# Where the next tile's query and key/value products stand in the first attention of a decoder layer

## The chip, the cores and the metric

The kernel runs on one core of a Trainium2 chip. What is measured is the device time of one execution in microseconds (us); lower is better. The core has five engines that run side by side, each through its own list of instructions in order: TensorE (PE in the profile; PEld is its weight load), VectorE (DVE), ScalarE (ACT), GpSimd (POOL) and SyncE (SP), which here issues most of the DMAs. They meet only at semaphores: an instruction can wait until a counter that other instructions raise has reached a value.

## The reference

One decoder layer on x of 16 x 64 rows of 512 numbers, in fp32: a self-attention, a cross-attention to a context, and a gated product, each followed by `layernorm(x + ...)`. The change touches the first of them only:

```
xq = rope((x @ Wq).reshape(b, 64, 32, 16))          # 32 heads of 16
xk = rope((x @ Wk).reshape(b, 64, 8, 16))           # 8 key heads, each used by 4 query heads
xv = (x @ Wv).reshape(b, 64, 8, 16)
scores = einsum('bqhd,bkhd->bhqk', xq, repeat(xk, 4)) / 4
probs  = softmax(where(causal, scores, -inf))
out    = einsum('bhqk,bkhd->bqhd', probs, repeat(xv, 4)).reshape(b, 64, 512) @ Wo
x      = layernorm(x + out)
```

`rope` turns each pair of numbers of a head by an angle that depends on the row's place.

## The kernel before

**Tiles.** The 1024 rows are cut into 8 tiles of 128 rows, two sequences of 64 each. The first attention runs one step per tile, `tile_steps(i)` for i = 0 to 7; steps 2 to 6 are a loop, the others are written out. Each of the five engines has its own `tile_steps`, and the order of calls in it is the order on that engine; nothing else orders the work. After step 7 comes a passage into the cross-attention, which the change doesn't touch.

**Precision.** Products are made in three passes: every operand is split into a high part (rounded by a ScalarE copy) and a low part (the rest, by a subtraction on VectorE or GpSimd), and high x high, high x low and low x high are summed. So each product of four 128-row chunks has 12 matmuls, and most tiles of data pass a pair of instructions, a copy named `..._high` or `copy` and a subtraction named `low`.

**Three tiles are in work at once.** Step i handles tile i up to its scores and softmax, tile v = i - 1 from its last probabilities to its output product, and tile w = i - 2 in its residual sum and layernorm. The calls that matter, by engine:

- TensorE: `b_stage` is the query product (12 matmuls of 512 columns, line 432) into bank 1, `kv_stage` the key/value product (12 of 256 columns, L413) into bank 2. `pt_stage(v, u)` turns the probabilities of unit u (0 to 3; a unit is a quarter of a tile's scores) in banks 3 and 4 (L451). `a_stage(i + 1)` turns the next x tile in bank 1 (L423). `qk_stage` turns queries and keys in six groups of four transposes (L487) that take banks 0, 3 and 4 in turn. `s_stage` makes scores, units 0 and 1 first, 2 and 3 later (L511). `pv_stage` is probabilities times values (L463), `x1_stage` turns the normed tile w (L523), `wo_stage` is the output product of tile v into bank 0 (L413, 12 matmuls of 512 columns).
- VectorE: `rope_q` (three instructions, L1317 to L1320) and `rope_k` (L1328 to L1331) read the products from banks 1 and 2. `q_low`, `p_low`, `x_low`, `at_low`, `x1_low` are subtractions that share L1300. `masked_max` is a masked copy of scores (L1382) and a maximum (L1384); `total` is a sum of exponentials (L1388) and a reciprocal. `add1(w)` (L1353) adds the output product in bank 0 to x; `stats1`, `moments1` and `norm1` are the layernorm.
- ScalarE: `p_high`, `x_high`, `at_high`, `x1_high`, the two copies that spread queries and keys over `stack_q` and `stack_k`, the copy `v_raw`, the six evictions of the turned queries and keys (semaphore `s_qke`), and `expo`, the exponentials (L876).
- GpSimd: `sub` subtracts the maximum (L1136), `norm` multiplies by the reciprocal (L1141), and two sums finish rope (L1154 for queries, semaphore `s_qs`; L1158 for keys, `s_ks`).

**Waits around the change.** `qk_stage` begins with two waits on TensorE, which hold all its six groups:

```
pe.wait_ge(s_ql, t + 1)          # q_low of this tile
if tile_stages(t)[2]:
    pe.wait_ge(s_res, t - 1)     # add1 of tile t - 2
```

The second is there because the first group of transposes writes bank 0, in which the output product of tile t - 2 lies until `add1` has read it. The second and third group wait for `p_low` of units 2 and 3, whose transposes lie in banks 3 and 4. `pt_stage` of units 2 and 3 waits for `p_low` of units 0 and 1, for the same banks. The fourth group waits for the first eviction, the fifth for the second, the sixth for the third, and the first scores for the third.

## Time and profile before

| | us |
|---|---|
| three runs | 827.94, 832.75, 835.98 |
| their median | 832.75 |
| the profiled execution | 829.94 |
| its span, first to last instruction | 828.1 |

The profiled execution is 1.8 us longer than its span. The first attention takes the first 22% of the span: its loop steps follow each other every 20.3 us, from about 57 to 159 us, and the passage into the cross-attention begins at about 180 us. The rows below are from the page of this execution and from views of its trace. A timeline row gives the start in us from the span's start, the length in us, the engine, the line, the operation, what it writes and reads, and, in brackets, how long the engine had been idle before it and what released it. Starts of instructions that follow each other on an engine are a little closer than their lengths, since one's end overlaps the next one's start.

### The profile page before, as it was taken

How to read it: one execution, taken by the hardware profiler on the slowest of the kernel's cores; microseconds unless marked ns; L12 is line 12 of the kernel's file. 1: busy time of each engine (PE TensorE's matmuls, PEld its weight loads, DVE VectorE, ACT ScalarE, POOL GpSimd, SP SyncE). 2: the span in 40 equal slices, each digit the busy share in tenths (PEclk: the TensorE clock that was granted, in tenths of full speed). 3: DMA queues.
4: the chain of work that ended last, by engine and by line, in shares of the span. 5: the costliest groups of instructions: out<-in, count | busy, mean ns of one | idle time of the engine just before them, and what ended most of it. 6: DMA issues, size and time to landing. Idle time of an engine off the chain costs nothing.

```text
span 828.1 us, 15482 instructions
## 1 busy us (share of the span) xinstructions
PE 763.8 (92%) x5504; PEld 688.7 (83%) x5504; DVE 626.5 (76%) x1172; ACT 317.2 (38%) x652; POOL 402.1 (49%) x422
## 2 busy tenths in 40 slices
PE   4689998899899999999999999999999999998792
PEld 3577777789799998999999899999989999996662
DVE  4778888877887777687777668768767876876967
ACT  4455555553443324233243324334333333322403
POOL 7566666664454445444543535454453554532124
PEclk9899999999999999999999999999999999999997
DMA  9600004012432222133122223212232221112002
GB/s 237 140 17 17 16 16 117 3 55 52 103 105 75 51 78 78 39 73 88 55 51 76 77 50 91 85 25 51 76 94 58 76 76 25 26 42 86 1 1 102
DMA packets 104047, 53.49 MB, mean 65 GB/s; under 512 B 80208, under 2 KB 89552, under 8 KB 104016
## 3 DMA queue, kind: packets, MB, share of 16 engines
q1 hardware_dynamic: 103184, 51.51, 24.1%
q10 hardware_dynamic: 576, 1.05, 0.4%
q0 software_dynamic: 256, 0.52, 0.2%
q8 instruction: 19, 0.31, 0.2%
q14 instruction: 12, 0.10, 0.0%
HBM read 32.62 MB, written 2.10 MB: 42 GB/s over the span
## 4 chain that ended last, share of the span: by engine, by line
PE 69%; DVE 16%; issue 7%; POOL 3%; ACT 2%; DMA 1%; SPq 1%; DVEq 0%; POOLq 0%
PE bank L413 30%; PE bank L640 18%; DVE arena_r L1300 4%; PE s_bank L654 4%; PE s_bank L656 2%; PE bank L463 2%; PE bank L624 2%; PE bank L487 2%; DVE small L1388 2%; DVE arena_f L1382 1%; PE s_bank L624 1%; DMA arena_f<-in_L_attn_Wo 1%; POOL arena_f L1215 1%; PE s_bank L487 1%; PE bank L633 1%
## 5 line engine op out<-in xcount | busy, mean ns | idle before, releaser
L413 PE MATMUL bank<-arena_r 128*128 128x256 f32 (+1 forms) x2580 | 354.6, 294 | 2.6 <-DVE arena_r L1300 1.8
L413 PEld LDWEIGHTS bank<-arena_r 128*128 128x128 f32 x2580 | 328.3, 191 | 18.4 <-issue 2.9
L838 ACT ACTIVATE arena_r<-bank 128x256 fp32r<-128x256 f32 (+2 forms) x251 | 105.7, 458 | 234.4 <-PE bank L607 99.1
L640 PE MATMUL bank<-arena_r 128*128 128x512 f32 x768 | 192.2, 399 | 1.1 <-DVE arena_r L1300 1.0
L640 PEld LDWEIGHTS bank<-arena_r 128*128 128x128 f32 x768 | 140.1, 189 | 28.3 <-issue 1.7
L1300 DVE TENSOR_TENSOR arena_r<-bank,arena_r 128x256 fp32r<-128x256 f32 (+2 forms) x219 | 100.8, 487 | 57.2 <-ACT arena_r L838 57.0
L838 ACT ACTIVATE arena_r<-arena_f 128x512 fp32r<-128x512 f32 (+2 forms) x177 | 103.1, 637 | 89.0 <-DMA arena_f<-arena_f 73.7
L1300 DVE TENSOR_TENSOR arena_r<-arena_f,arena_r 128x512 fp32r<-128x512 f32 (+1 forms) x113 | 114.1, 1023 | 20.7 <-ACT arena_r L838 20.7
L1182 POOL TENSOR_TENSOR arena_f<-arena_f 128x256 f32<-128x256 f32 x64 | 54.2, 847 | 91.6 <-DVE arena_f L1460 91.5
L1210 POOL TENSOR_TENSOR arena_f<-arena_f,small 128x512 f32<-128x512 f32 x32 | 33.4, 1045 | 117.2 <-DVE small L1523 117.2
L1215 POOL TENSOR_TENSOR arena_f<-arena_f,small 128x512 f32<-128x512 f32 x32 | 44.2, 1380 | 68.1 <-DVE small L1529 68.1
L1486 DVE TENSOR_TENSOR arena_f<-bank,arena_f 128x512 f32<-128x512 f32 x64 | 43.9, 685 | 25.6 <-PE bank L640 25.6
L838 ACT ACTIVATE arena_f<-s_bank 128x512 f32<-128x512 f32 (+1 forms) x34 | 20.3, 598 | 98.9 <-PE s_bank L656 96.8
L656 PE MATMUL s_bank<-arena_r 128*128 128x64 f32 x256 | 57.9, 245 | 0.0
L654 PE MATMUL s_bank<-arena_r 128*128 128x128 f32 x256 | 57.2, 295 | 0.0
L838 ACT ACTIVATE arena_r<-s_bank 128x512 fp32r<-128x512 f32 (+1 forms) x98 | 51.8, 529 | 1.0 <-PE s_bank L487 0.7
L1183 POOL TENSOR_TENSOR arena_f<-arena_f 128x256 f32<-128x256 f32 x64 | 50.1, 783 | 0.0
L656 PEld LDWEIGHTS s_bank<-arena_r 128*128 128x128 f32 x256 | 49.1, 192 | 1.2
L654 PEld LDWEIGHTS s_bank<-arena_r 128*128 128x128 f32 x256 | 49.1, 192 | 1.2
L1517 DVE TENSOR_TENSOR arena_f<-s_bank,arena_f 128x512 f32<-128x512 f32 x32 | 22.1, 692 | 36.7 <-ACT arena_f L838 36.7
L1136 POOL TENSOR_TENSOR arena_f<-arena_f,small 128x512 f32<-128x512 f32 x32 | 34.8, 1087 | 30.7 <-DVE small L1384 30.7
L1300 DVE TENSOR_TENSOR arena_r<-s_bank,arena_r 128x512 fp32r<-128x512 f32 x82 | 47.4, 580 | 1.2 <-ACT arena_r L838 0.9
(134 smaller groups left out, 1029.8 us busy)
## 6 DMA issues: line engine op xcount, KB each, us to landing
arena_f<-arena_f SPq DMA_DIRECT2D x128, 128.0 KB, 2.5
arena_f<-in_L_xattn_Wq SPq DMA_DIRECT2D x8, 1024.0 KB, 5.5
arena_f<-in_L_xattn_Wo SPq DMA_DIRECT2D x8, 1024.0 KB, 5.5
arena_f<-in_x SPq DMA_DIRECT2D x8, 256.0 KB, 2.8
arena_f<-in_x SPq DMA_DIRECT2D x1, 2048.0 KB, 16.9
arena_f<-in_L_xattn_Wk SPq DMA_DIRECT2D x8, 256.0 KB, 2.9
arena_f<-in_L_xattn_Wv SPq DMA_DIRECT2D x8, 256.0 KB, 3.2
arena_f<-in_ctx SPq DMA_DIRECT2D x8, 256.0 KB, 3.1
```

The lines of the kernel that those rows point to most:

```text
L413: mm = pe.matmul(bank, lhs(a, c), rhs(b, c), start=(c == 0 and n == 0), stop=(c == chunks - 1 and n == 2))
L640: mm = pe.matmul(BO2[i][:], at2[a][:, h, i * P:(i + 1) * P], w2o_s[b][:, h, :], start=(h == 0 and n == 0), stop=(h == HG - 1 and n == 2))
L654: pe.matmul(BS2[h][:, at:at + 2 * S], high, kT2[:, :, b * S:(b + 1) * S], start=True, stop=False, skip_group_check=True)
L656: mm = pe.matmul(BS2[h][:, at + S:at + 2 * S], low_, kT2[:, 0, b * S:(b + 1) * S], start=False, stop=True, skip_group_check=True)
L838: act.activation(dst, src, ACT.Copy).then_inc(done, 1)
L1136: pool.tensor_tensor(cut(p1[u], b=8, k=S), cut(sc1[u % 2], b=8, k=S), bcast(mx1[u], 2, S), ALU.subtract).then_inc(s_sub, 1)
L1182: pool.tensor_tensor(u1q[:, 0, j, :], u1q[:, 0, j, :], u2q[:, 1, j, :], ALU.subtract).then_inc(c_qs, 1)
L1183: pool.tensor_tensor(u1q[:, 1, j, :], u1q[:, 1, j, :], u2q[:, 0, j, :], ALU.add).then_inc(c_qs, 1)
L1210: pool.tensor_tensor(cut(p2, b=8, k=S), cut(sc2, b=8, k=S), bcast(mx2, 2, S), ALU.subtract).then_inc(c_sub, 1)
L1215: pool.tensor_tensor(cut(p2, b=8, k=S), cut(p2, b=8, k=S), bcast(sm2, 2, S), ALU.mult).then_inc(c_pn, 1)
L1300: dve.tensor_tensor(dst, src, f32(high), ALU.subtract).then_inc(done, 1)
L1486: dve.tensor_tensor(y, banks[6 + i][:], y, ALU.add).then_inc(c_acc, 1)
```

## The change

The query product of tile i + 1 moves on TensorE from the start of step i + 1 to the middle of step i, behind the first scores; the key/value product from between the probability transposes of step i + 1 to the end of step i. The first tile's two products stand ahead of step 0. The other engines are put in an order to match: on VectorE `rope_q(i + 1)` goes between `total(i, 0)` and `total(i, 1)` of step i, `rope_k` comes after `p_low` of unit 0, `add1` comes after `p_low` of unit 3, and `at_low` after both totals; on GpSimd the query sum moves with `rope_q`; on ScalarE the x copy comes before the second eviction instead of before the fourth, `at_high` comes after the exponentials of units 0 and 1, and the probability copies are spread otherwise. No instruction is added or removed but for waits.

```diff
@@ TensorE, tile_steps(i)
-                b_stage(i, start)
                 if old:
                     pt_stage(v, 0)
                     pt_stage(v, 1)
-                if old:
-                    pe.wait_ge(s_cp, 4 * i)
-                kv_stage(i, start)
-                if old:
                     pt_stage(v, 2)
                     pt_stage(v, 3)
                 if following:
...
                 qk_stage(i, start)
                 s_stage(i, (0, 1), start)
+                if following:
+                    b_stage(i + 1, False)
                 if old:
                     pv_stage(v, 0, not oldest)
                     pv_stage(v, 1, not oldest)
...
                 s_stage(i, (2, 3), start)
                 if old:
                     wo_stage(v, i, not oldest)
+                if following:
+                    if oldest:
+                        pe.wait_ge(s_x1l, w + 1)
+                    else:
+                        pe.wait_ge(s_rk, i + 1)
+                        pe.wait_ge(s_vr, i + 1)
+                    kv_stage(i + 1, False)
...
             pe.wait_ge(s_init, 3)
+            b_stage(0, True)
+            kv_stage(0, True)
             tile_steps(0)
@@ ScalarE, tile_steps(i)
                 if old:
                     p_high(v, 0, not oldest)
-                    p_high(v, 1, not oldest)
                 act.wait_ge(s_qs, i + 1)
...
                 if old:
-                    p_high(v, 2, not oldest)
+                    p_high(v, 1, not oldest)
+                act.wait_ge(s_rk, i + 1)
+                if old:
+                    act.wait_ge(s_vl, i)
+                copy(v_raw, banks[2][:, KV1:2 * KV1], s_vr)
                 act.wait_ge(s_ks, i + 1)
...
                 if old:
+                    p_high(v, 2, not oldest)
                     p_high(v, 3, not oldest)
...
-                    if j == 3 and following:
+                    if j == 1 and following:
                         x_high(i + 1)
...
-                if old:
-                    at_high(v, not oldest)
                 expo(i, 0)
+                expo(i, 1)
...
-                expo(i, 1)
+                if old:
+                    at_high(v, not oldest)
@@ GpSimd, tile_steps(i)
                 if old:
                     norm(v, 2)
-                pool.wait_ge(s_rq, i + 1)
-                pool.tensor_tensor(t1q, t1q, t2q, ALU.add).then_inc(s_qs, 1)
-                if old:
                     norm(v, 3)
...
                 norm(i, 0)
+                if following:
+                    sum_q1(i + 1)
@@ VectorE, tile_steps(i)
                 if old:
                     total(v, 2)
-                rope_q(i, not old)
-                if old:
                     total(v, 3)
                     p_low(v, 0)
+                rope_k(i, not old)
+                if old:
                     p_low(v, 1)
-                rope_k(i, not old)
...
-                if oldest:
-                    add1(w)
                 q_low(i)
                 if old:
                     p_low(v, 2)
                     p_low(v, 3)
                 if oldest:
+                    add1(w)
                     stats1(w)
...
+                total(i, 0)
+                if following:
+                    rope_q(i + 1, False)
+                total(i, 1)
                 if old:
                     at_low(v)
-                total(i, 0)
                 masked_max(i, 2, not old)
-                total(i, 1)
```

How the order on the engines moves, at the places that matter. In the changed kernel lines of VectorE stand 10 lower (L1300 is L1310, L1353 is L1363), and rows named REGISTER_ALU or ISA are wait or register instructions.

VectorE in the loop, before, from `p_low` of unit 1 over `rope_k`, `add1` (L1353) and `q_low` to the layernorm's statistics:

```order
L1300 TENSOR_TENSOR arena_r<-s_bank,arena_r 128x2x2x128
L1328 TENSOR_TENSOR arena_f<-bank,rope 128x128
L1330 SCALAR_TENSOR_TENSOR arena_f<-bank,rope 128x64
L1331 TENSOR_TENSOR arena_f<-bank,rope 128x64
L1353 ISA
L1353 TENSOR_TENSOR arena_f<-bank,arena_f 128x512
L1300 TENSOR_TENSOR arena_r<-arena_f,arena_r 128x32x32
L1300 TENSOR_TENSOR arena_r<-bank,arena_r 128x2x2x128
L1300 TENSOR_TENSOR arena_r<-s_bank,arena_r 128x2x2x128
L1358 BN_STATS small<-arena_f 128x6
```

And with the change:

```order
L1335 REGISTER_ALU
L1338 TENSOR_TENSOR arena_f<-bank,rope 128x128
L1340 SCALAR_TENSOR_TENSOR arena_f<-bank,rope 128x64
L1341 TENSOR_TENSOR arena_f<-bank,rope 128x64
L1344 REGISTER_ALU
L1310 TENSOR_TENSOR arena_r<-s_bank,arena_r 128x2x2x128
L1310 TENSOR_TENSOR arena_r<-arena_f,arena_r 128x32x32
L1310 TENSOR_TENSOR arena_r<-bank,arena_r 128x2x2x128
L1310 TENSOR_TENSOR arena_r<-s_bank,arena_r 128x2x2x128
L1363 ISA
L1363 TENSOR_TENSOR arena_f<-bank,arena_f 128x512
L1368 BN_STATS small<-arena_f 128x6
```

`add1` (now L1363) has moved from ahead of `q_low` to behind it and behind `p_low` of units 2 and 3; `rope_k` has moved ahead of `p_low` of unit 1.

VectorE at the start of a loop step, before: the sums of units 2 and 3 of tile v, with `rope_q` between them.

```order
L1388 TENSOR_REDUCE small<-arena_f 128x8
L1390 RECIPROCAL small<-small 128x8
L1314 REGISTER_ALU
L1317 TENSOR_TENSOR arena_f<-bank,rope 128x512
L1319 SCALAR_TENSOR_TENSOR arena_f<-bank,rope 128x256
L1320 TENSOR_TENSOR arena_f<-bank,rope 128x256
L1387 REGISTER_ALU
L1388 TENSOR_REDUCE small<-arena_f 128x8
L1390 RECIPROCAL small<-small 128x8
```

And with the change:

```order
L1398 TENSOR_REDUCE small<-arena_f 128x8
L1400 RECIPROCAL small<-small 128x8
L1397 REGISTER_ALU
L1398 TENSOR_REDUCE small<-arena_f 128x8
L1400 RECIPROCAL small<-small 128x8
L1344 REGISTER_ALU
L1310 TENSOR_TENSOR arena_r<-bank,arena_r 128x2x2x128
```

The two sums now stand side by side, with only their reciprocals between.

TensorE in the loop, before, from the last first score (L511) over `pv_stage` (L463) and `x1_stage` (L523) to the later scores:

```order
L511 MATMUL bank<-arena_r 128x64
L463 MATMUL bank<-arena_r 128x256 x24
L523 MATMUL bank<-ident,arena_f 128x128 x4
L503 REGISTER_ALU
L505 REGISTER_ALU
L511 MATMUL s_bank<-arena_r 128x64
```

And with the change:

```order
L511 MATMUL bank<-arena_r 128x64
L432 MATMUL bank<-arena_r 128x512 x12
L463 MATMUL bank<-arena_r 128x256 x24
L523 MATMUL bank<-ident,arena_f 128x128 x4
L503 REGISTER_ALU
L505 REGISTER_ALU
L511 MATMUL s_bank<-arena_r 128x64
```

The 12 matmuls of the query product (L432) now stand between the two groups of scores.

## Rows read from the trace of the kernel before

**Rows 1.** the page: busy us of the span (instructions), and clock in 40 slices

```profile
PE 763.8 (92%) x5504; PEld 688.7 (83%) x5504; DVE 626.5 (76%) x1172; ACT 317.2 (38%) x652; POOL 402.1 (49%) x422
...
PEclk9899999999999999999999999999999999999997
```

**Rows 2.** busy time by engine in one loop step, clock, DMA share, GB/s

```profile
81.09:101.41 20.32, 18.53 (x140) 15.92 (x140) 18.01 (x36) 11.89 (x22) 12.93 (x14) 1.00 0.08 16
```

**Rows 3.** timeline, VectorE, that step: start, length, work [idle before, releaser]

```profile
87.30 0.69 DVE L1300 TENSOR_TENSOR arena_r<-bank,arena_r 128x512 fp32r<-128x512 f32 x1 [1.35 <-ACT arena_r L838]
...
88.71 0.75 DVE L1382 COPY_PREDICATED arena_f<-causal,s_bank 128x512 f32<-128x512 int32 x1 [0.44 <-PE bank L511]
...
92.20 0.69 DVE L1300 TENSOR_TENSOR arena_r<-bank,arena_r 128x512 fp32r<-128x512 f32 x1 [0.17 <-ACT arena_r L838]
```

**Rows 4.** timeline, VectorE, early in the next step, around the residual sum

```profile
102.65 0.68 DVE L1353 TENSOR_TENSOR arena_f<-bank,arena_f 128x512 f32 x1
...
103.25 1.22 DVE L1300 TENSOR_TENSOR arena_r<-arena_f,arena_r 128x1024 fp32r<-128x1024 f32 x1
...
104.38 0.69 DVE L1300 TENSOR_TENSOR arena_r<-bank,arena_r 128x512 fp32r<-128x512 f32 x1
...
104.98 0.68 DVE L1300 TENSOR_TENSOR arena_r<-s_bank,arena_r 128x512 fp32r<-128x512 f32 x1
```

**Rows 5.** timeline, TensorE, from the transposes to the next tile's query product

```profile
84.20 1.26 PE L487 MATMUL bank<-ident,arena_r 128*128 128x128 f32 x8 [0.75 <-DVE arena_r L1300]
...
86.83 0.63 PE L487 MATMUL s_bank<-ident,arena_r 128*128 128x128 f32 x4
...
87.39 0.29 PE L511 MATMUL s_bank<-arena_r 64*128 64x64 f32 x1
...
88.40 3.13 PE L463 MATMUL bank<-arena_r 128*128 128x256 f32 x24
...
91.90 0.29 PE L511 MATMUL s_bank<-arena_r 64*128 64x64 f32 x1
...
95.86 2.89 PE L432 MATMUL bank<-arena_r 128*128 128x512 f32 x12
```

**Rows 6.** timeline, ScalarE, same step, the six evictions and the x copy

```profile
84.89 1.20 ACT L838 ACTIVATE arena_r<-bank 128x512 fp32r<-128x512 f32 x2 [0.62 <-PE bank L487]
...
86.16 0.60 ACT L838 ACTIVATE arena_r<-s_bank 128x512 fp32r<-128x512 f32 x1
86.67 1.57 ACT L838 ACTIVATE arena_r<-bank 128x512 fp32r<-128x512 f32 x3
```

**Rows 7.** timeline, VectorE, at a step's end and the next one's start

```profile
93.75 0.76 DVE L1382 COPY_PREDICATED arena_f<-causal,s_bank 128x512 f32<-128x512 int32 x1
...
94.55 0.69 DVE L1384 TENSOR_REDUCE small<-arena_f 128x8 f32<-128x512 f32 x1
...
97.42 0.69 DVE L1384 TENSOR_REDUCE small<-arena_f 128x8 f32<-128x512 f32 x1
98.02 0.68 DVE L1388 TENSOR_REDUCE small<-arena_f 128x8 f32<-128x512 f32 x1
...
98.90 0.69 DVE L1317 TENSOR_TENSOR arena_f<-bank,rope 128x512 f32<-128x512 f32 x1
...
100.17 0.68 DVE L1388 TENSOR_REDUCE small<-arena_f 128x8 f32<-128x512 f32 x1
```

**Rows 8.** timeline, GpSimd, at the same place

```profile
95.50 1.04 POOL L1136 TENSOR_TENSOR arena_f<-arena_f,small 128x512 f32<-128x512 f32 x1
...
96.50 1.04 POOL L1141 TENSOR_TENSOR arena_f<-arena_f,small 128x512 f32<-128x512 f32 x1
...
98.18 1.05 POOL L1136 TENSOR_TENSOR arena_f<-arena_f,small 128x512 f32<-128x512 f32 x1 [0.64 <-DVE small L1384]
```

**Rows 9.** timeline, ScalarE, at the same place, the fourth exponential

```profile
99.26 0.63 ACT L876 ACTIVATE arena_f<-arena_f 128x512 f32<-128x512 f32 x1 [2.06 <-POOL arena_f L1136]
```

**Rows 10.** busy time by engine and clock in a start-up stretch

```profile
20.00:22.00 2.00, 0.00 (x0) 0.00 (x0) 2.00 (x4) 1.26 (x3) 0.82 (x1) 0.50 1.04 361
```

More of the change, by code:

```diff
@@ L894, in tile_steps @@
                 if old:
+                    p_high(v, 2, not oldest)
                     p_high(v, 3, not oldest)
-                act.wait_ge(s_rk, i + 1)
-                if old:
-                    act.wait_ge(s_vl, i)
-                copy(v_raw, banks[2][:, KV1:2 * KV1], s_vr)
                 if not following:
@@ L1142, in norm, with sum_q1 @@
                                    ALU.mult).then_inc(s_pn, 1)
+            def sum_q1(t):
+                pool.wait_ge(s_rq, t + 1)
+                pool.tensor_tensor(t1q, t1q, t2q, ALU.add).then_inc(s_qs, 1)
             def root1(w):
@@ L1241, in _ @@
             pool.wait_ge(s_init, 3)
+            sum_q1(0)
             tile_steps(0)
@@ L1396, in tile_steps @@
                     total(v, 2)
-                rope_q(i, not old)
-                if old:
                     total(v, 3)
                     p_low(v, 0)
+                rope_k(i, not old)
+                if old:
                     p_low(v, 1)
-                rope_k(i, not old)
-                if not old:
+                else:
                     for h in range(HG):
@@ L1445, in _ @@
             dve.wait_ge(s_init, 3)
+            rope_q(0, True)
             def ctx_low(t):
```

## The prediction

> **What bounds the kernel now.** I read the page first, then the busy time of one loop step, then the timelines of VectorE, TensorE, ScalarE and GpSimd in that step. The page says that TensorE is busy for 92% of the span and VectorE for 76%, and that the clock of TensorE is near full throughout [rows 1]; but this is a mean over stages. In the first attention a step takes 20.32 us, in which TensorE is busy for 18.5 and VectorE for 18.0 [rows 2], and both wait now and then. So neither's own work sets the step alone; what does is a loop over both, and it is read best on VectorE, which has next to no room: its waits in the step are 1.35, 0.44 and 0.17 us [rows 3], together 1.96. All else, 18.36 us, is work that it does after the change as well. The step after the change is therefore 18.36 us plus the waits of VectorE in the new order, and these I work out one by one.
>
> The first two waits are one thing. VectorE has handed over everything that the turned queries and keys need, and until the first scores come it has only the statistics, the x subtraction and the moments to do. The first wait is for the x copy, the second for the scores.
>
> **The change, part by part.**
>
> *The path to the first scores.* TensorE's six groups of transposes stand behind a wait for the residual sum `add1` (its bank 0). Before, that sum stands ahead of `q_low` and two `p_low`, so it is done 1.13 us before `q_low` is [rows 4] and its wait costs nothing. Now it is the last of the four. From its start the way to the first scores is: the sum is 0.68 long [rows 4] and what it releases starts some 0.05 later, 0.73; first transposes to first eviction, 84.20 to 84.89, 0.69 [rows 5, 6]; the eviction 0.60, then, newly in front of the second one, the x copy, 0.50 (of three in 1.57, the last two starting 0.5 apart), then the second 0.60, then the third, 86.16, after which the sixth group starts at 86.83, 0.67 [rows 5, 6]: 2.37; sixth group to scores 0.56 and scores to the masked copy, 87.39 to 88.71, 1.32 [rows 3, 5]. Sum 5.67 us.
>
> In that time VectorE has: the sum itself 0.60 (102.65 to 103.25) [rows 4], the statistics, taken like other instructions of 512 elements as 0.60 (104.38 to 104.98) [rows 4], and the x subtraction with the moments, 87.30 to 88.71 less the wait of 0.44, 0.97 [rows 3]. That is 2.17. It waits 3.50 us, where it waited 1.79. Plus 1.71 us a step. Of this the x copy is 0.5, the place of the sum the rest.
>
> *The end of a step.* The exponentials of unit 3 come at the end of a chain over GpSimd: mask copy of unit 2 to its maximum 0.80, the maximum 0.69 [rows 7], 0.07 to GpSimd (97.42 + 0.69 to 98.18) [rows 7, 8], subtraction 1.00, normalising of unit 1 1.00, subtraction of unit 3 to its exponential 1.08 [rows 8], the exponential 0.63 and 0.04 to VectorE [rows 9]. Sum 5.31 from the mask copy to the sum of unit 3. GpSimd is free when that maximum comes, also with the query sum ahead of it. VectorE's work between the two was 93.75 to 100.17, 6.42 us, with `rope_q` (98.90 to 100.17, 1.27) and `total` of unit 1 (as 98.02 to 98.90, 0.88) in it [rows 7]. Both are gone from there, 4.27 is left. A wait of 1.04 us that did not exist: `rope_q` was its cover. The later work on GpSimd and ScalarE in the following step hangs on it too.
>
> *The middle.* TensorE now has scores 1.01 (87.39 to 88.40), query product, probabilities times values with the turn of w, 3.50 (88.40 to 91.90), and then the later scores. The query product is 2.89 long with some 0.2 of it beside what follows, 2.7 [rows 5]. That is 7.2 us from first to later scores instead of 4.5. VectorE's work between the two mask copies was 88.71 to 93.75 less 0.17, 4.87 [rows 3, 7]; `rope_q` 1.27 and `total` 0.88 are added, 7.02. So the product is covered, and a wait of 0.2 takes the place of the old 0.17 for `at_high`, which has more time now. This part of the change does what its words say: TensorE has a product to do while the softmax runs.
>
> *The start of a step.* The query product, 2.7 us, leaves TensorE's way to the probability transposes, and the key/value product too. But the transposes of units 2 and 3 wait for `p_low` of units 0 and 1, and these for VectorE's sums, so TensorE idles there. The keys' rope comes some 0.6 earlier in the order; keys are ready before `p_low` of unit 3 is, and buy nothing. The probability copies of units 2 and 3 come a little late: 0.1 us.
>
> *DMAs.* None is added. The value copy, whose four DMAs follow, comes earlier; the x load follows `a_stage` as before, with most of a step to land. At nothing; were a load late, its place is `a_stage`, a step later.
>
> Waits per step: 3.50 + 1.04 + 0.2 + 0.1 = 4.84 against 1.96, plus 2.9; walking the five orders through with the same durations, where waits can overlap, gives 2.8. The same walk for the order before gives 20.2 where the rows have 20.32. I take 2.8 for each of the six steps with a residual sum, steps 2 to 7: 16.8 us. Steps 0 and 1 have none: there the x copy costs 0.5 each, and the bare end of the step 0.5 and 1.0, 2.5. That `rope_q` counts to one step earlier adds in step 0 what it takes from step 7. Sum 19.3, less about 0.4, since step 2 follows a step that still had the shorter path: 19 us. The cross-attention and the rest keep their order and shift by it.
>
> **The sum** against the profiled execution: 829.94 + 19 = 849. The median of the three runs, 832.75, is 2.8 higher and would give 852. I say 850.
>
> Bounds. The durations of rows lie within a few hundredths of each other from step to step; a path over a dozen hand-overs at 0.05 to 0.1 each may be 0.5 longer or shorter per step, so 15 to 23 us. The runs before spread by 8 us.
>
> **A rule against a row.** The waits of VectorE repeat in each step, and the longest, 1.35, is for the x copy [rows 3], which now comes two evictions earlier. Taken alone that is a gain of up to 1.35 in seven steps, 9.5 us. But behind it stands the wait for the scores, and what is not waited for the one is waited for the other: the time from the hand-over to the scores sets both, and the copy lengthens it. The Trainium skill (Perfetto Trace Analysis, Optimization Strategy) says to find the gaps on the engine to be optimised, see which semaphore holds it, and make that dependency start sooner or end faster. By that alone the time would be about 820.
>
> **The rivals.**
>
> *Faster.* `rope_q` in the middle and the early x copy fill VectorE's waits, and it runs through. It has 18.36 us of work; the step would fall by up to 1.96, over eight steps 15.7 us: 814. For it speaks that VectorE is at 18.0 of 20.32 [rows 2] and that the middle comes out nearly without a wait. It decides where the path from `add1` to the scores falls below 5.67 - 3.50 + 0.8, some 3 us, and nothing in the rows is that short: evictions and scores alone are 1.8 and 1.32. 0.06, with 820 of the x copy alone in it.
>
> *Little.* The residual sum isn't the last to release the transposes, because the waits at the end of a step delay `q_low` or the key subtraction on GpSimd more than I see, or the `p_low` do. Then the first group starts a little over a microsecond earlier, and the step is 21.7: about 10 us more in all, 840 to 842. Against it: the sum stands behind both `p_low` in VectorE's order. 0.13, half of it within 1%.
>
> *Nothing.* The engines' slack absorbs it, 830 to 834; the two waits on which I count would both have to be covered. 0.03.
>
> *The clock.* TensorE's clock was 0.50, that is 1.2 GHz, in a stretch of the start-up in which TensorE had no work at all [rows 10]. TensorE now waits about 2 us at once in two places per step, before unit 2's transposes and before the queries', where it had 0.75 before the queries' [rows 5]. If the clock fell in every loop step, the 7.2 us from scores to scores would near 14, and the step would be 7 us longer still: 890 or more. Over the loop step the clock was at full speed with that wait in it [rows 2, 5]. 0.03. The Trainium skill (TensorE: Matmul & The Clock Gate, HAM oscillation) says that gaps between bursts of matmuls bring the clock down to half; no row before shows it for gaps this short.
>
> **Chances.** The forecast, 843 to 858, has 0.75; the rivals 0.25. About 1% is what a measurement of this kernel can tell from no change. Faster by over 1%: 0.06. Within 1%: half of *little* and *nothing*, 0.09. Slower: 0.85. The range reaches down to take in most of *little*, and up to the upper bound of the sum on the slower runs: 840 to 859.
>
> **What the profile would show.** Step length 23.1 us in the loop, from one first exponential to the next. On TensorE a wait of about 2 us before the first query transposes, released by the residual sum (L1363). On VectorE waits of about 1.4 and 2.0 us before the x subtraction and the first mask copy, a new one of 1.0 before the sum of unit 3, released by ScalarE's exponential, and 0.2 before the mask copy of unit 2. The query product between the two groups of scores, hidden. TensorE's clock at 1.00. I'm wrong if the transposes are released by something else than the sum, if the step is under 21 us, or if waits turn up in the cross-attention, which I take as unchanged.

## The result, and the profile after

| | before | after |
|---|---|---|
| median (lowest to highest), us | 832.73 (827.94 to 835.98) | 856.65 (855.94 to 858.95) |
| span of the profiled execution, us | 828.1 | 854.1 |
| mean clock of TensorE in it | 0.988 | 0.966 |

The ratio is 1.0297, with a 95% interval of 1.0243 to 1.0351: slower by 3%, where 850, or 2% slower, was forecast. Each median is that of four executions. The profiled executions differ by 26.0 us. Where it went is read best from one mark per tile: the start of VectorE's reciprocal behind the sum of unit 3.

| step, from mark to mark | before | after | difference |
|---|---|---|---|
| start of the program to the first mark | 39.55 | 39.88 | 0.33 |
| step 1 | 20.68 | 22.07 | 1.39 |
| steps 2 to 6 | 20.34, 20.31, 20.33, 20.32, 20.23 | 23.06, 24.15, 23.93, 23.92, 23.88 | 17.41 |
| step 7 | 22.43 | 27.89 | 5.46 |
| passage, cross-attention, gated product | 643.9 | 645.3 | 1.4 |

So 24.6 of the 26.0 us lie in the first attention, which is where the forecast had them. But only the first of the five loop steps has the length that it gave, 23.1. The page of the changed kernel, as [rows 1] of before (busy us by engine; clock in 40 slices):

```profile
PE 776.1 (91%) x5504; PEld 702.6 (82%) x5504; DVE 626.6 (73%) x1172; ACT 318.0 (37%) x652; POOL 401.3 (47%) x422
...
PEclk9899899999999999999999999999999999998997
```

VectorE's work is what it was, 626.6 against 626.5. TensorE runs the same 5504 matmuls and is busy for 12.3 us more: the same work at another speed. The busy time by engine and the clock in four loop steps of the changed kernel show where (length, then PE, PEld, DVE, ACT, POOL, clock, DMA share, GB/s, as [rows 2]):

```profile
61.23:84.29 23.06, 18.66 (x142) 15.94 (x140) 18.09 (x36) 11.86 (x23) 13.06 (x14) 1.00 0.08 16
84.29:108.44 24.15, 20.57 (x140) 18.26 (x140) 18.16 (x35) 12.00 (x23) 12.98 (x14) 0.86 0.07 14
108.44:132.37 23.93, 19.70 (x140) 17.53 (x140) 18.08 (x36) 11.88 (x23) 12.97 (x14) 0.93 0.07 14
132.37:156.29 23.92, 19.68 (x140) 17.50 (x140) 18.08 (x36) 11.87 (x23) 12.96 (x14) 0.93 0.35 101
```

In the first step the clock is 1.00 and TensorE's work that of before, 18.66 against 18.53; in the others the clock is below 1.00 and the work 1.0 to 1.9 longer. VectorE in the first of these steps, at full clock, all its waits over 0.1 us (to be read against [rows 3, 7]):

```profile
68.78 0.69 DVE L1310 TENSOR_TENSOR arena_r<-bank,arena_r 128x512 fp32r<-128x512 f32 x1 [1.11 <-ACT arena_r L844]
...
71.68 0.74 DVE L1392 COPY_PREDICATED arena_f<-causal,s_bank 128x512 f32<-128x512 int32 x1 [1.93 <-PE bank L511]
...
75.20 0.69 DVE L1398 TENSOR_REDUCE small<-arena_f 128x8 f32<-128x512 f32 x1 [0.21 <-ACT arena_f L882]
...
78.92 0.75 DVE L1392 COPY_PREDICATED arena_f<-causal,s_bank 128x512 f32<-128x512 int32 x1 [0.17 <-PE bank L511]
...
84.29 0.69 DVE L1398 TENSOR_REDUCE small<-arena_f 128x8 f32<-128x512 f32 x1 [1.08 <-ACT arena_f L882]
```

These are the waits for the x copy, for the first scores, for the exponential of unit 0, for the later scores, and at the step's end for the exponential of unit 3. TensorE in the step two further on, from the transposes of units 2 and 3 to those of the queries:

```profile
110.08 0.65 PE L451 MATMUL bank<-ident,arena_f 128*128 128x128 f32 x4 [1.74 <-DVE arena_r L1310]
111.18 0.65 PE L451 MATMUL s_bank<-ident,arena_f 128*128 128x128 f32 x4 [0.45 <-DVE arena_r L1310]
...
114.17 1.94 PE L487 MATMUL bank<-ident,arena_r 128*128 128x128 f32 x8 [1.90 <-DVE arena_f L1363]
115.90 1.06 PE L487 MATMUL s_bank<-ident,arena_r 128*128 128x128 f32 x4
...
119.46 3.03 PE L432 MATMUL bank<-arena_r 128*128 128x512 f32 x12
```

The wait of 1.90 is released by the residual sum, L1363, where 0.75 for `q_low` stood before [rows 5]. And the transposes behind it are slow: eight take 1.94 us and four 1.06, where eight took 1.26 and four 0.63 [rows 5]. The same stretch in windows of 1 us (columns as above):

```profile
112.00:113.00 1.00, 0.27 (x3) 0.03 (x1) 1.00 (x3) 0.58 (x2) 1.00 (x1) 1.00 0.32 33
113.00:114.00 1.00, 0.00 (x0) 0.00 (x0) 1.00 (x2) 0.00 (x0) 0.31 (x1) 0.97 0.16 17
114.00:115.00 1.00, 0.83 (x4) 0.86 (x5) 0.71 (x2) 0.00 (x0) 0.00 (x0) 0.50 0.75 82
...
116.00:117.00 1.00, 1.00 (x7) 1.00 (x6) 0.15 (x1) 0.78 (x2) 0.00 (x0) 0.50 0.00 0
117.00:118.00 1.00, 1.00 (x9) 0.99 (x8) 0.79 (x3) 1.00 (x3) 0.10 (x1) 0.83 0.00 0
```

The clock goes to 0.50, 1.2 GHz, at the end of the pause, and comes back some 3 us later, on the path to the first scores. In the step before this one, from 84.29, it fell earlier: behind the wait of 1.74 alone the next four transposes took 1.11 us instead of 0.65, and that step is the longest, 24.15. Last, TensorE in step 7 and the start of the passage:

```profile
185.86 1.94 PE L487 MATMUL bank<-ident,arena_r 128*128 128x128 f32 x8 [2.37 <-DVE arena_f L1363]
...
198.45 4.61 PE L413 MATMUL bank<-arena_r 128*128 128x512 f32 x12 [2.71 <-DVE arena_r L1310]
...
204.00 5.99 PE L413 MATMUL bank<-arena_r 128*128 128x256 f32 x48
```

Here both the wait before the queries' transposes (2.37) and one before the output product (2.71, for `at_low`, 0.25 in the kernel before) are followed by slow matmuls: the output product took 3.03 us before and takes 4.61.

### The profile page after: what moved, and what is told of

It is laid out like the page before. It is cut to its first block, busy times and chain, and to the rows that moved or that the text cites. A ratio compares the mean times of both kernels' runs of the same rounds, so it can differ in the third digit from the quotient of the medians.

```text
span 854.1 us, 15484 instructions
## 1 busy us (share of the span) xinstructions
PE 776.1 (91%) x5504; PEld 702.6 (82%) x5504; DVE 626.6 (73%) x1172; ACT 318.0 (37%) x652; POOL 401.3 (47%) x422
## 4 chain that ended last, share of the span: by engine, by line
PE 68%; DVE 13%; issue 8%; POOL 6%; ACT 2%; DMA 2%; SPq 1%; POOLq 0%; DVEq 0%; ACTq 0%
PE bank L413 28%; PE bank L644 17%; DVE arena_r L1310 4%; PE s_bank L658 4%; PE bank L487 2%; PE s_bank L660 2%; PE bank L628 2%; PE bank L463 2%; PE bank L432 2%; POOL arena_f L1142 2%; PE s_bank L511 1%; PE s_bank L628 1%; DMA arena_f<-in_L_attn_Wo 1%; POOL arena_f L1224 1%; PE bank L611 1%
## 5 line engine op out<-in xcount | busy, mean ns | idle before, releaser
L1310 DVE TENSOR_TENSOR arena_r<-bank,arena_r 128x256 fp32r<-128x256 f32 (+2 forms) x219 | 100.5, 485 | 56.6 <-ACT arena_r L844 56.3
L1310 DVE TENSOR_TENSOR arena_r<-arena_f,arena_r 128x512 fp32r<-128x512 f32 (+1 forms) x113 | 112.8, 1010 | 20.9 <-ACT arena_r L844 20.9
L1310 DVE TENSOR_TENSOR arena_r<-s_bank,arena_r 128x512 fp32r<-128x512 f32 x82 | 47.5, 580 | 0.6
## 6 DMA issues: line engine op xcount, KB each, us to landing
arena_f<-in_x SPq DMA_DIRECT2D x1, 2048.0 KB, 17.4
```

The costliest lines, as they stand in the source:

```text
L1310: dve.tensor_tensor(dst, src, f32(high), ALU.subtract).then_inc(done, 1)
```

## The experiments

Two theories. **Order:** each loop step is 2.7 us longer by its order, from three causes: the residual sum, which is the last to release the transposes; the x copy in front of the second eviction; and the end of the step without `rope_q`. **Clock:** the rest of the loop's loss, some 0.9 us per step, comes from the pauses on TensorE, after which its clock is at 1.2 GHz. The rivals: something else than the clock lengthens the steps (the clock being a symptom); and for each cause of order, that its wait is hidden and the wait behind it the real one. "Walk" stands for the walk of the five orders by hand, with durations from rows, as in the prediction. Each ratio is to executions of the kernel before that were measured together with that experiment. Where the intervals of two ratios overlap, as those of the changed kernel and experiment 1, of 1 and 5, or of 2 and 3, the total does not tell the two apart, and the reading rests on the steps.

| experiment | median, us | ratio to before (95%) | loop steps, us | clock in them |
|---|---|---|---|---|
| 1 unused transposes | 852.83 | 1.025 (1.0221 to 1.0279) | 23.03 to 23.06 | 1.00 |
| 2 sum ahead of `q_low` | 846.92 | 1.0186 (1.0158 to 1.0214) | 21.9, 22.5 in two | 1.00, lower in two |
| 3 sum between two totals | 845.25 | 1.0147 (1.0113 to 1.018) | 21.3, 22.2 in one | 1.00, lower in one |
| 4 x copy late | 857.69 | 1.0302 (1.0278 to 1.0327) | 23.9 | 0.93 |
| 5 = 1 and 4 | 850.69 | 1.0233 (1.0206 to 1.026) | 22.5 | 1.00 |
| 6 before, sum late | 847.51 | 1.0188 (1.0161 to 1.0215) | 21.8 in two, 23.3 in three | 1.00 or 0.91 to 0.94 |
| 7 before, x copy early | 834.88 | 1.0037 (1.0018 to 1.0056) | 20.7 | 1.00 |
| 8 other order | 834.64 | 1.0025 (1.0003 to 1.0047) | 20.0 | 1.00 |
| 9 = 2 and 4 | 847.68 | 1.0215 (1.018 to 1.0251) | 21.5, 22.0 in one | 1.00, lower in one |
| 10 last step | 856.67 | 1.033 (1.0296 to 1.0363) | as after | as after |
| 11 = 8, both ends mended | 833.22 | 1.0038 (1.002 to 1.0056) | 20.0 | 1.00 |
| 12 = 11, clock held at the ends | 831.89 | 1.0012 (1.0000 to 1.0025) | 20.0 | 1.00 |

**1, 4 and 5: the clock, and the x copy.** The first adds 12 transposes that nothing reads in each of the two pauses:

```diff
                     pt_stage(v, 1)
+                    filler(12)      # 12 x pe.transpose(BO[:, 0:P], ident, ident)
                     pt_stage(v, 2)
...
+                if old:
+                    filler(12)
                 qk_stage(i, start)
```

> The changed kernel with 12 transposes of the identity into a bank that is free (bank 7) put on TensorE twice per step from step 1 on: before the transposes of unit 2's probabilities and before the query transposes, where TensorE stood idle for 1.7 to 1.9 us. Their results are not used. Clock theory (the steps take 23.9 instead of the 23.06 of the one step at full clock because TensorE's pauses let its clock fall to 1.2 GHz at the query transposes): the clock stays at 1.00 in the loop, steps are 23.0 to 23.1, and the time falls by 4 to 5 us to 851 to 853. Rival (the 0.9 us come from VectorE, GpSimd and hand-overs): no change, or up to 1 us per step slower by TensorE's 24 more transposes, 857 to 864.

The fourth puts the x copy back to its place, and the fifth does both:

```diff
-                    if j == 1 and following:
+                    if j == 3 and following:
                         x_high(i + 1)
```

> The changed kernel with one edit: the x copy on ScalarE stands before the fourth eviction again instead of before the second. Theory (it lengthens the way to the first scores by its 0.5 us): step 0.5 us shorter in all eight steps, 3 to 4 us, 852 to 854. Rival (an early x copy is a gain, since VectorE waits for it): slower by up to 4 us, 857 to 861.

> The changed kernel with the 24 unused transposes per step that held the clock, and the x copy before the fourth eviction again. Theory (the x copy costs its 0.5 us on the way to the first scores; the run without the transposes hid that, because the clock fell in each step): clock 1.00 in the loop, steps of 22.5 us against 23.03, some 3 to 4 us faster than the changed kernel with the transposes alone, 848 to 850. Rival (the x copy isn't on the path): steps of 23.0, 852 to 853.

With the unused transposes TensorE has more to do and the steps are shorter, 23.03 where 23.0 to 23.1 was expected. A loop step of experiment 1 by busy time, and TensorE in it:

```profile
110.93:133.96 23.03, 21.09 (x167) 18.57 (x166) 18.06 (x36) 11.79 (x23) 12.99 (x13) 1.00 0.07 14
```

```profile
110.37 1.47 PE L538 MATMUL bank<-ident 128*128 128x128 f32 x12
112.27 0.65 PE L451 MATMUL bank<-ident,arena_f 128*128 128x128 f32 x4 [0.42 <-DVE arena_r L1318]
...
114.29 1.47 PE L538 MATMUL bank<-ident 128*128 128x128 f32 x12
116.36 1.06 PE L487 MATMUL bank<-ident,arena_r 128*128 128x128 f32 x8 [0.60 <-DVE arena_f L1371]
117.26 0.60 PE L487 MATMUL s_bank<-ident,arena_r 128*128 128x128 f32 x4
```

The waits are released by the same instructions as in the changed kernel, and the work behind them is at full speed: eight transposes 1.06 us, four 0.60. So the clock was the cause and no symptom, and costs 0.87 us in a usual loop step (23.06 against 23.93), in four of the five. The total fell by 3.8 us from the changed kernel's median.

Experiment 4 missed what the order theory gave it, 852 to 854: it is no faster than the changed kernel. VectorE in a loop step of it:

```profile
119.00 0.69 DVE L1310 TENSOR_TENSOR arena_r<-bank,arena_r 128x512 fp32r<-128x512 f32 x1 [3.52 <-ACT arena_r L844]
120.37 0.75 DVE L1392 COPY_PREDICATED arena_f<-causal,s_bank 128x512 f32<-128x512 int32 x1 [0.41 <-PE bank L511]
```

The wait only changed its name, 3.52 and 0.41 for 2.00 and 1.94 in the changed kernel at the same clock. ScalarE in the same step, the second and third eviction:

```profile
116.77 0.60 ACT L844 ACTIVATE arena_r<-bank 128x512 fp32r<-128x512 f32 x1 [0.26 <-PE bank L487]
117.63 0.60 ACT L844 ACTIVATE arena_r<-s_bank 128x512 fp32r<-128x512 f32 x1 [0.26 <-PE s_bank L487]
```

Where the x copy stood, ScalarE now waits for transposes at 1.2 GHz: beside these the copy had cost nothing. All five loop steps have this clock, the first too, although its pauses on TensorE (1.46, 0.51 and 1.86) are those of the changed kernel's first loop step, which kept 1.00. With the clock held, experiment 5, the copy's place is worth 0.52 us a step (23.03 to 22.51), where the walk has 0.5; its total, 850.69, is a little above the 848 to 850 expected. A cost of order could not be seen alone while the clock fell in the same stretch.

**2 and 3: the residual sum.**

```diff
+                if oldest:
+                    add1(w)         # 3: between total(v, 2) and total(v, 3)
                 q_low(i)
                 if old:
                     p_low(v, 2)
                     p_low(v, 3)
                 if oldest:
-                    add1(w)
                     stats1(w)
```

> The changed kernel with one edit: the residual sum stands ahead of q_low again, as before the change. Theory (the sum is the last release of the query transposes): step 21.8 at full clock, 7.5 us less by the walk of the orders, and a few us more if the shorter pause keeps the clock up: 845 to 849. Rival (the transposes wait for p_low of units 2 and 3 anyway): 855 to 857, no change. Rival (the loss is the query product between the two groups of scores): no change.

> The changed kernel with one edit: the residual sum between the sums of unit 2 and unit 3 at the start of a step. It leaves the path to the query transposes as in the run above, and it also covers 0.6 us of the 1.04 us wait for the exponentials of unit 3. Theory of the bare end of the step: 3 us faster than with the sum ahead of q_low (step 21.2), 842 to 846. Rival (that wait is not on the path, it is hidden by later waits): same as with the sum ahead of q_low.

At full clock a step of experiment 2 is 21.9, 1.17 below 23.06. TensorE in one:

```profile
84.73 0.65 PE L451 MATMUL bank<-ident,arena_f 128*128 128x128 f32 x4 [1.71 <-DVE arena_r L1310]
...
87.48 1.26 PE L487 MATMUL bank<-ident,arena_r 128*128 128x128 f32 x8 [0.56 <-DVE arena_r L1310]
```

The sum no longer releases the transposes, `q_low` does, after 0.56. The pause of 1.71 stands alone and the clock is at 1.00 in this step; in two others it did fall. Experiment 3 puts the sum into the hole at the step's end: the wait there goes from 1.08 to 0.44, and the step from 21.9 to 21.3. So that wait is on the path too, and the sum placed in it costs nothing.

**6 and 7: one move of the change alone, in the kernel before.**

```diff
-                if oldest:
-                    add1(w)         # 6
                 q_low(i)
                 if old:
                     p_low(v, 2)
                     p_low(v, 3)
                 if oldest:
+                    add1(w)
                     stats1(w)
...
-                    if j == 3 and following:
+                    if j == 1 and following:    # 7
                         x_high(i + 1)
```

> The kernel before with one edit: the residual sum stands behind both p_low of units 2 and 3, before the statistics, as in the change. Nothing else is moved. Theory (it is then the last release of the query transposes): step 21.5 instead of 20.3, 7.3 us more by the walk, and more if the clock falls: 838 to 843. Rival (the sum matters only together with the moved products): within 1 us of the kernel before.

> The kernel before with one edit: the x copy stands before the second eviction. Theory (the way to the first scores is 0.5 us longer, VectorE's wait for the x copy turns into a longer one for the scores): step 20.7 to 20.8, 3 us more, 834 to 836. Rival (VectorE's largest wait, 1.35 us for the x copy, goes away): up to 9 us less, 822 to 828.

Experiment 6, TensorE and then VectorE in a loop step:

```profile
88.60 1.12 PE L487 MATMUL bank<-ident,arena_r 128*128 128x128 f32 x8 [2.53 <-DVE arena_f L1353]
```

```profile
92.17 0.69 DVE L1300 TENSOR_TENSOR arena_r<-bank,arena_r 128x512 fp32r<-128x512 f32 x1 [2.89 <-ACT arena_r L838]
94.33 0.75 DVE L1382 COPY_PREDICATED arena_f<-causal,s_bank 128x512 f32<-128x512 int32 x1 [1.18 <-PE bank L511]
```

Moving one instruction by three places costs 15.5 us against the kernel before, more than the 838 to 843 expected: 1.46 us a step by order (20.33 to 21.79; walk 1.3), and another 1.5 in the three steps in which the clock fell. It did so behind this one pause (1.00 in the window from 88 to 89 us, 0.50 from 90 to 92); one step earlier the same pause, 2.53 at 66.80, had kept it. Step 7 is 26.41 us against 22.43. The expectation named the clock and priced it too low.

Experiment 7 sets the rule against the rows. VectorE in a loop step:

```profile
105.97 0.69 DVE L1300 TENSOR_TENSOR arena_r<-bank,arena_r 128x512 fp32r<-128x512 f32 x1 [0.26 <-ACT arena_r L838]
...
108.87 0.75 DVE L1382 COPY_PREDICATED arena_f<-causal,s_bank 128x512 f32<-128x512 int32 x1 [1.94 <-PE bank L511]
```

The longest gap, 1.35 [rows 3], is down to 0.26, and the one behind it up from 0.44 to 1.94: 1.79 together before, 2.20 now, and the step is 0.4 longer. Step 7 is 23.59 against 22.43; there the clock is at 0.50 in the windows from 166 to 169 us, behind a wait of 1.10 that the kernel before has too, at full clock. The Trainium skill (Perfetto Trace Analysis, Optimization Strategy) has one find the gap and make the work that ends it start sooner; that alone gave about 820, and measured is 834.88. The gap went, the path did not.

**8: the products moved, the three causes not taken along.** The query and key/value products stand where the change puts them, but the sum comes first in the step, `rope_k` between the two totals, and the x copy before the fourth eviction. Other calls were moved with them, as the expectation lists: probability copies, the key sum, the x transposes, the layernorm of tile w and its turn. In part, against the kernel before:

```diff
+                if oldest:
+                    add1(w)
                 if old:
                     total(v, 2)
-                rope_q(i, not old)
+                rope_k(i, not old)
...
-                if oldest:
-                    add1(w)
                 q_low(i)
...
+                if following:
+                    rope_q(i + 1, False)
+                total(i, 0)
+                total(i, 1)
                 if old:
                     at_low(v)
```

> A version that keeps the moved products and takes out the three costs: residual sum ahead of the sum of unit 2 and the keys' rope between the sums of units 2 and 3 (both cover the wait for the exponentials of unit 3), x copy before the fourth eviction, probability copies of units 0 and 1 together, the key sum on GpSimd ahead of the normalising of unit 3, the x transposes between those of units 1 and 2, the moments and the layernorm of tile w ahead of the first mask copy, the query's rope ahead of the sum of unit 0, and the turn of w behind the later scores. Theory: by the walk the step is 19.8 us, and the whole 0.8 us below the kernel before: 829 to 834 if the clock holds, with 1 to 4 us more if it falls. Rival (moving the products themselves costs, through TensorE's bare start of a step): step over 21 us, 840 or more.

VectorE's waits over 0.1 us in a loop step:

```profile
109.35 0.69 DVE L1311 TENSOR_TENSOR arena_r<-bank,arena_r 128x512 fp32r<-128x512 f32 x1 [0.84 <-ACT arena_r L845]
110.76 0.75 DVE L1393 COPY_PREDICATED arena_f<-causal,s_bank 128x512 f32<-128x512 int32 x1 [0.26 <-PE bank L511]
...
117.02 0.69 DVE L1311 TENSOR_TENSOR arena_r<-bank,arena_r 128x512 fp32r<-128x512 f32 x1 [0.53 <-ACT arena_r L845]
```

Together 1.63 against 1.96 [rows 3], and the step is 20.03 against 20.33 (walk 19.8 against 20.2). So the products can stand at their new places without a cost to the loop step, once the three causes are left out. Whether the 0.3 us a step are theirs or come from the other calls that moved is not shown. The whole is not faster: step 1 is 21.64 against 20.68 and step 7 is 24.13 against 22.43. (One of its ten executions took 1898.42 us, for which nothing here gives a cause; it is left out of the ratio.)

**9: the sum early and the x copy late.**

> The changed kernel with the residual sum ahead of q_low and the x copy before the fourth eviction, both as before the change; what is left of the change is the place of the two products, of the query's rope and of the rest. Theory (what is left costs the bare end of each step, about 1 us, and the last step): step 21.3 at full clock, 8 us above the kernel before, plus 2 to 5 us of clock: 842 to 845. Rival (nothing is left once the two are undone): within 2 us of the kernel before.

The loop steps are 21.5 at full clock, where 21.3 was expected, and 1.57 below 23.06, where the sum alone gave 1.17 and the copy alone 0.52. What is left to 20.33 is 1.16, about the wait of 1.08 at the step's end, which is there in this experiment too. The total missed its 842 to 845 by 3 us: step 7 is 28.84, with the output product at 5.49 us behind a wait of 2.71.

**10: the last step.** `at_high` and `at_low` stand in step 7 where they stood before.

```diff
+                if not following:
+                    at_high(v, False)
                 expo(i, 0)
                 expo(i, 1)
...
-                if old:
+                if following and old:
                     at_high(v, not oldest)
```

> The changed kernel with at_high ahead of the exponentials and at_low ahead of the sums in step 7 alone, as before the change. In the changed kernel TensorE stood idle for 2.7 us before the output product of tile 6 there, which then took 4.6 us at 1.2 GHz instead of 3.0, and VectorE waited for it. Clock theory (a good part of the last step's excess is that product at half clock behind the pause): 2 to 3 us faster than the changed kernel, 853 to 855. Rival (order alone, at full clock): 0.4 us.

TensorE at its end and in the passage:

```profile
195.95 3.06 PE L413 MATMUL bank<-arena_r 128*128 128x512 f32 x12 [0.25 <-DVE arena_r L1312]
...
201.97 0.63 PE L451 MATMUL s_bank<-ident,arena_f 128*128 128x128 f32 x4 [2.52 <-POOL arena_f L1149]
202.35 7.49 PE L413 MATMUL bank<-arena_r 128*128 128x256 f32 x48
```

Step 7 is 25.64 instead of 27.89, as meant, and the total does not move: the pause and the low clock come one product later, and 48 matmuls take 7.49 us where they took 5.99. The time gained was given back within 10 us.

**11 and 12: a kernel with both ends mended.** The eleventh is 8 with step 0 in its old order and step 7 as in 10; the twelfth adds unused transposes, three times 8 in step 1 and 18 in the passage:

```diff
             pt_stage(v, 0)
+            filler(18)
             pt_stage(v, 1)
```

> The reordered version with its two ends mended: in step 7 at_high and at_low as before the change, and in step 0 the query product of tile 1 behind the later scores, its rope between the sums of step 1, as before the change. In the reordered version the loop steps took 20.03 us against 20.33, but the steps 0 and 1 lost 3.4 us and the last 1.7. Theory (these losses are from the two ends): 3 to 5 us faster than the reordered version, 828 to 832, 0 to 3 us below the kernel before. Rival (the loop's 0.3 us per step are lost again in the passage): no faster than the kernel before.

> The reordered version with its ends mended, and unused transposes of the identity into bank 7 in four of TensorE's pauses outside the loop: 8 each at three places of step 1, and 18 before the transposes of unit 1 in the passage to the cross-attention. In the version without them TensorE's clock was at 1.2 GHz for some 6 us from 40 us on and for 3 us from 180 us on, after pauses of 1.1 to 1.2 us in a row and of 2.4 us, and the first query products of the cross-attention took 7.5 us instead of 6.0. Clock theory: the clock stays at 1.00 at both places and the time falls by 2 to 3 us to 830 to 831.5, within 1 us of the kernel before or a little below. Rival (the time lost outside the loop is not the clock's): 832 to 834 as without them.

TensorE in the passage, in experiment 11 and then in 12:

```profile
179.15 0.63 PE L451 MATMUL s_bank<-ident,arena_f 128*128 128x128 f32 x4 [2.38 <-POOL arena_f L1151]
179.53 7.49 PE L413 MATMUL bank<-arena_r 128*128 128x256 f32 x48
```

```profile
179.01 2.13 PE L538 MATMUL bank<-ident 128*128 128x128 f32 x18
181.59 0.63 PE L451 MATMUL s_bank<-ident,arena_f 128*128 128x128 f32 x4 [0.45 <-POOL arena_f L1164]
181.97 6.00 PE L413 MATMUL bank<-arena_r 128*128 128x256 f32 x48
```

In the kernel before the same wait is 1.77 and the product 6.00. Experiment 11 ends the first attention 0.5 us earlier than the kernel before (mark at 183.69 against 184.19), and loses 1.5 in the product. Experiment 12 holds the clock there. Neither is faster than the kernel before, 1.0038 and 1.0012, and neither total reached what was expected, 828 to 832 and 830 to 831.5. The loop gives 0.3 us in each of its five steps, and step 7 gives 0.5; the start takes part of it back, with step 1 at 21.60 and 21.38 against 20.68 and the clock at 0.50 in the windows from 40 to 46 us of experiment 11, where the kernel before has 1.00. In its profiled execution experiment 12 also reached its first mark only at 42.59, where 11 did at 40.00. More is lost behind the first attention: from the last mark to the end are 643.9 us in the kernel before, 646.9 in experiment 11 and 647.0 in 12. About half of this in experiment 12 arises late in the cross-attention, behind a wait of TensorE of 2.19 us: the clock is at 0.50 in the windows from 757 to 763 us, and 12 matmuls take 5.00 us that take 3.53 in the kernel before. The kernel before waits 2.17 us there, and its clock falls too, for a shorter time. The expectation had looked for a low clock in two places only. What makes the first mark later by 2 to 3 us in some profiled executions (it was at 42.64 in experiment 1 and 41.97 in 8) was not tried.

## Why the prediction was right, and where it was short

| term | forecast, us | measured, us |
|---|---|---|
| steps 0 and 1 | 2.5 | 0.33 + 1.39 = 1.7 |
| steps 2 to 6 by order | 5 x 2.8 - 0.4 = 13.6 | 5 x 2.72 = 13.6 |
| steps 3 to 6, clock | 0 | 17.4 - 13.6 = 3.8 |
| step 7 | 2.8 | 5.5 |
| the rest | 0 | 1.4 |
| sum | 19 | 26.0 |

The time fell inside the stated range, 840 to 859, and that was in part luck. The two medians differ by 23.9 us and the profiled executions by 26.0, both above the 15 to 23 of the sum's own bounds; the range holds 856.65 because its upper end was counted from the slowest execution of the kernel before, 835.98. The mechanism of the loop step was right; 6.5 us of clock and step 7 were missing.

**What bounds the kernel** was read rightly: the step is VectorE's work, which did not change, plus its waits. The waits over 0.1 us add up to 4.50 where 4.84 was forecast, and all else to 18.56 where 18.36 was taken as fixed, so that two small misses cancel in part in the 2.72 that were measured for 2.8. **The path to the first scores:** two waits of 3.50 together were forecast and 3.04 measured (1.11 and 1.93) at full clock, with 0.21 more at the sum of unit 0, which was not named. The residual sum as last releaser was shown by experiments 2 and 6, the x copy's 0.5 by 5 and 7. Of the statement that the plus of 1.71 is 0.5 for the copy and 1.2 for the sum, both parts held as costs of the step: 0.52 and 1.17, each undone alone, though these two waits themselves grew by 1.25 only. **The end of a step:** 1.04 forecast, 1.08 measured, and experiment 3 showed that it counts. **The middle:** 0.2 forecast, 0.17 measured; the query product is hidden, and experiment 8 shows that the loop step need not be longer for it. **Faster by the x copy alone** was refuted by 7, *little* by the releaser of the wait, and *faster* and *nothing* by the time itself.

**The step that failed is "TensorE's clock at 1.00".** The mechanism had been seen as a rival, with 0.03, since at a wait of 0.75 before the queries the clock was full. That row said nothing of waits of 1.9, and the trace of before had no loop step to bound them. Outside the first attention it had rows that did, so that "no row before shows it for gaps this short" holds of the rows that were read and not of the trace. TensorE late in the cross-attention of the kernel before, and where the gated product begins:

```profile
751.94 0.44 PE L607 MATMUL bank<-ident,arena_f 128*128 128x128 f32 x2 [2.17 <-POOL arena_f L1215]
753.40 0.99 PE L624 MATMUL bank<-arena_r 64*128 64x256 f32 x6 [0.81 <-DVE arena_r L1300]
...
767.95 0.43 PE L767 MATMUL bank<-ident,arena_f 64*128 64x64 f32 x4 [2.38 <-DVE arena_r L1300]
...
770.77 0.62 PE L624 MATMUL bank<-arena_r 64*128 64x256 f32 x6 [0.82 <-DVE arena_r L1300]
```

Behind the pause of 2.17 the clock is at 0.73, 0.50, 0.50 and 0.56 in the windows of 1 us from 753 on, and six matmuls take 0.99 us; behind that of 2.38 it stays at 1.00 and they take 0.62. So pauses of this length could cost some 3 us at half clock, and did not always. The price was wrong too, on the other side: 7 us a step supposed that the clock would stay low from scores to scores. It is back before the scores, and costs 0.9 us where the step's path runs over the slow transposes. A clock that falls for a few microseconds per pause belonged into the bounds of the sum, and not only into a rival at 890.

**Step 7 was mis-sized.** It was taken as one more loop step. But `at_low` now comes after both totals, and the last step has no query product in the middle that keeps TensorE at work: the output product waited 2.71 us instead of 0.25 and then ran at the low clock. Experiment 10 took 2.25 us off the step. The statement on `at_high`, "more time now", holds in the loop only. That *the cross-attention is unchanged* held to 1.4 us of 645. Of these, 1.1 arise late in it and in the gated product, where TensorE waits 3.19 us (to 776.76) and 2.38 us (to 793.46) and its clock is at 0.50 behind both; the kernel before waits 2.17 and 2.38 at these places, as shown above. What made the first of the two longer is open. From the last mark to the end the fourteen traces have 643.9 to 647.9 us, so a difference of a few microseconds between two totals can lie there.

## What to carry to other kernels

Where engines run their lists in order, look for the last releaser of each wait, not for the first long gap: an instruction that moves by three places costs nothing or a microsecond a step, depending on whether it frees a buffer that others write, and a gap that is filled may only move to the next wait. Where a change makes TensorE pause, add to the price of the pause the speed of what stands behind it. And price the first and last step by their own rows, since what covers a wait in the loop is missing there.

## What the runs showed of the hardware

TensorE's clock can fall after short pauses, and did not each time. In the changed kernel the loop step with pauses of 1.46 and 1.86 us, with some 2.2 us from one to the next, kept 1.00; in experiment 4 the step with the same pauses fell, and its eight transposes took 1.94 us. The step shown above, with 1.74 and 1.90, fell to 0.50 for some 3 us. In experiment 2 a step with 1.71 and 0.56 kept it, and so did one with 1.75 and 0.57, while one with 1.73 fell behind that pause alone. In experiment 6 a pause of 2.53 kept it in the first loop step and not in the second. After a pause of 2.38, 2.52 or 2.71 us the product behind it ran slow in each case shown in the experiments; the kernel before kept 1.00 after 1.77 and after 2.38 (767.95), and not after 2.17. The price is that of the work at 1.2 instead of 2.4 GHz for a few microseconds: 0.9 us in a loop step, 1.5 in the 48 matmuls of the passage, 1.6 in the output product. The same order at the same place fell in some steps and not in others (experiments 2, 3, 6 and 9), so that from 1.7 to 2.5 us the length of a pause alone did not decide it here. The Trainium skill (TensorE: Matmul & The Clock Gate, A second HAM failure mode: psum-queue depth-cycling) tells of a kernel in which short idles between groups of matmuls make the clock swing; the windows above agree, with 1.00 at 112 us, 0.50 from 114 and 1.00 again by 118.

Unused transposes held the clock at next to no cost, where TensorE had idle time for them: 24 per step took TensorE from 19.7 to 21.1 us of busy time and the step from 23.93 to 23.03 (experiment 1).
